# A four-layer graph network on one core: the third layer's weights' pass with its SyncE and ScalarE queues written out, and other points at which gathered rows are spilled

## The reference

```python
e = ei_all[idx_i] + ej_all[idx_j]
e = jnp.where(e > 0, e, LEAKY_SLOPE * e)
alpha = _segment_softmax(e.astype(jnp.float32), idx_j, n)
msgs = alpha[:, None] * x[idx_j]
out = jax.ops.segment_sum(msgs, idx_i, num_segments=n)
return jax.nn.relu(out)
```

## Time and profile before

| what | value |
|---|---|
| median of 3 runs | 4589.87 us (4589.16 to 4594.28) |
| span of the profiled execution | 5974.2 us |
| time of the profiled execution itself | not recorded apart from its span |
| GpSimd busy over the span | 3220.8 us, 54% |
| TensorE busy over the span | 2467.8 us, 41% |
| VectorE busy over the span | 2086.7 us, 35% |
| the third layer's stage, first gather to the next layer's first | 2800.66 to 4639.86 us of the span |

### The profile page before, as it was taken

The page is one execution under the profiler, slowest core; times in us unless marked ns, Lnnn a source line. Parts: engine busy times, 40 slices in busy tenths (PEclk is TensorE's granted clock), DMA queues, the critical chain, the costliest instruction groups (busy, mean ns, idle before and its releaser), DMA issues. The chain is left out here.

```text
span 5974.2 us, 63099 instructions
## 1 busy us (share of the span) xinstructions
PE 2467.8 (41%) x16441; PEld 2221.3 (37%) x16441; DVE 2086.7 (35%) x5443; ACT 830.0 (14%) x2496; POOL 3220.8 (54%) x3391
## 2 busy tenths in 40 slices
PE   2344444444333333332766666454566222222221
PEld 1333333333233333331666666344455222222220
DVE  4344434444122222222444344355544122222223
ACT  0111212122000000000322222000001011001112
POOL 3555555554566666664344444545443666666664
PEclk7555555555555555555555555566666556555555
DMA  4222222222122222223333333455555344434443
GB/s 102 57 60 60 61 58 60 59 61 57 41 47 47 47 49 47 48 47 63 115 110 108 107 108 115 130 162 162 162 164 160 93 117 116 108 108 112 112 116 82
DMA packets 427122, 543.15 MB, mean 91 GB/s; under 512 B 116266, under 2 KB 291966, under 8 KB 426862
## 3 DMA queue, kind: packets, MB, share of 16 engines
q1 hardware_dynamic: 311618, 311.80, 17.7%
q0 software_dynamic: 108064, 223.63, 16.6%
q10 hardware_dynamic: 7344, 6.61, 0.4%
HBM read 403.82 MB, written 142.41 MB: 91 GB/s over the span
## 5 line engine op out<-in xcount | busy, mean ns | idle before, releaser
L523 POOL DMA_INDIRECT G<-table,IC x2496 | 2362.6, 947 | 1571.7 <-issue 832.5
L2412 POOL DMA_INDIRECT G<-table,IC x448 | 433.1, 967 | 580.9 <-ACT IC L2271 425.1
L2818 DVE TENSOR_TENSOR_SCAN GW<-BIG,GW,PS 128x512 f32<-128x512 bf16 x208 | 266.2, 1280 | 962.9 <-DMA BIG<-run_mask 620.8
L2412 POOL DMA_INDIRECT G<-table2c,IC x384 | 367.3, 956 | 407.0 <-DMA rows_ahead<-G 148.8
L2780 PE MATMUL PS<-IDENT,GW 128*128 128x128 f32 x840 | 192.5, 405 | 862.3 <-issue 481.4
L1360 PE MATMUL PS<-SEL,G 128*128 128x96 f32 x1664 | 372.1, 417 | 358.1 <-DVE SEL L556 217.1
L1032 PE MATMUL PS<-SEL,GW 128*128 128x96 f32 x1664 | 382.4, 419 | 291.6 <-DVEq L1095 158.9
L1360 PEld LDWEIGHTS PS<-SEL,G 128*128 128x128 f32 x1664 | 359.7, 327 | 365.5 <-DVE SEL L556 220.1
L2780 PEld LDWEIGHTS PS<-IDENT,GW 128*128 128x128 f32 x840 | 158.9, 215 | 887.3 <-issue 495.6
L1032 PEld LDWEIGHTS PS<-SEL,GW 128*128 128x128 f32 x1664 | 356.4, 322 | 304.3 <-DVEq L1095 165.3
L2426 PE MATMUL PS<-BIG 128*128 128x49 f32 x1680 | 387.4, 408 | 60.7 <-issue 31.8
(11 more groups left out here) (314 smaller groups left out, 3749.1 us busy)
## 6 DMA issues: line engine op xcount, KB each, us to landing
rows_ahead<-G SPq DMA_DIRECT2D x104, 520.0 KB
running_max<-BIG SPq DMA_DIRECT2D x105, 512.0 KB
G<-table,IC POOLq DMA_INDIRECT x2944
GW<-source_in_block SPq DMA_DIRECT2D x160, 256.0 KB
ROWSF<-edge_places SPq DMA_DIRECT2D x209, 192.0 KB
BIG<-run_mask SPq DMA_DIRECT2D x104, 256.0 KB
ROWSF<-rows_ahead SPq DMA_DIRECT2D x26, 520.0 KB
SELTF<-rows_ahead SPq DMA_DIRECT2D x26, 520.0 KB
```

The source lines that it names most:

```text
L523: pool.indirect_dma_start(out=G[:, b, u, 0:width], out_offset=None, in_=table, in_offset=bass.IndirectOffsetOnAxis(ap=IC[:, b * U + u:b * ...
L2412: pool.indirect_dma_start(out=GS[:, b, u, 0:width], out_offset=None, in_=table, in_offset=bass.IndirectOffsetOnAxis(ap=IC[:, b * U + u:b * ...
L2818: v.tensor_tensor_scan(RM[:, q, h * 512:(h + 1) * 512], MB[:, q, h * 512:(h + 1) * 512], PS[2 * q + h][:], before, ALU.min, ALU.max).then_ ...
```

## The change

It replaces the loops of `sp_sums` and `act_sums` by straight Python loops over all 104 groups, and with them the fixed places of the spills and index copies by a table `sums_plan`. Pair p now stands after group ceil((20.3 (p + 1) - 10) / 21.2 x 4) - 1, for as many pairs as fall inside the pass: pairs 0, 1, 2, 3 after groups 1, 5, 9, 13, pair 6 after group 24, and so on to pairs 25 and 26 after groups 97 and 101. That is 27 pairs in the pass, where it was 26. The plan of the message pass begins with pair 27 and counts from 20.3 x (p - 27), so each pair stands where the pair two before it stood. The wait for the column moves from ScalarE's queue to GpSimd's, between the last gather from `T2` and the first from `T2C`.

```diff
+            FIRST_TURN, LEAD, EARLY = 21.2, 10.0, 28
+            sums_plan, plan, place = {}, {}, 0
+            for pair in range(EARLY):
+                at = max(0, math.ceil((PAIR * (pair + 1) - LEAD) / FIRST_TURN * RING) - 1)
+                if at < GROUPS:
+                    sums_plan.setdefault((at // RING, at % RING), []).append(pair)
+            kept_early = sum(map(len, sums_plan.values()))
+            for pair in range(kept_early, GROUPS // 2):
                 latest = (pair // 2, 1) if pair % 2 else (pair // 2 - 1, 3)
-                while points[place][0] < PAIR * (pair - 25) and points[place][1:] < latest:
+                while points[place][0] < PAIR * (pair - EARLY + 1) and points[place][1:] < latest:
...
+            def sp_sums(sp, reg):
+                for turn in range(LAPS):
+                    for b in range(RING):
+                        i = edge(turn, b)
+                        sp.wait_ge(lo_hot, i + 2)
+                        sp.dma_start(LOB[:, 1 - b % 2, :], LOD[(i + 1) * L:(i + 2) * L].unsqueeze(0)
+                                     .to_broadcast([P, L])).then_inc(lo_in[1 - b % 2], 16)
+                        sp.wait_ge(row_hot, i + 1)
+                        sp.wait_ge(terms, i + 1)
+                        load_windows(sp, reg, i, b % 2, T2W, 3, row_in, win_in)
+                        for pair in sums_plan.get((turn, b), ()):
+                            for group in (2 * pair, 2 * pair + 1):
+                                spill(sp, group, group % RING, group // RING)
...
-                        sp_sums(sp, reg, 0, 1, False)
-                        sp_sums(sp, reg, 1, LAPS // 2, True)
-                        spill(sp, 50, 2, 12)
-                        spill(sp, 51, 3, 12)
+                        sp_sums(sp, reg)
...
-                def refill(act, turn, b):
-                    for pair in plan.get((turn, b), ()):
-                        if pair == 26:
-                            act.wait_ge(column_in, 32)
+                            refill(act, sums_plan.get((turn, b), ()))
+
+                def refill(act, some):
+                    for pair in some:
...
                         gather_turns(pool, 0, PICKED // RING, T2, D)
+                        pool.wait_ge(column_in, 32)
                         gather_turns(pool, PICKED // RING, LAPS, T2C, C)
```

More of the change, by code:

```diff
@@ L1 @@
+import math
 import numpy as np
@@ L2250, in layer2 @@
                       for tau in range(LAPS) for b in (1, 3)]
-            plan, place = {}, 0
-            for pair in range(26, GROUPS // 2):
+            FIRST_TURN, LEAD, EARLY = 21.2, 10.0, 28
[6 more added lines that the diff above has]
+            for pair in range(kept_early, GROUPS // 2):
                 latest = (pair // 2, 1) if pair % 2 else (pair // 2 - 1, 3)
-                while points[place][0] < PAIR * (pair - 25) and points[place][1:] < latest:
+                while points[place][0] < PAIR * (pair - EARLY + 1) and points[place][1:] < latest:
                     place += 1
@@ L2344, in _ @@
                     sp.nop()
[L2346 to L2370, removed]
@@ L2372, in refill, with act_sums @@
-                def refill(act, turn, b):
-                    for pair in plan.get((turn, b), ()):
-                        if pair == 26:
-                            act.wait_ge(column_in, 32)
+                def act_sums(act):
+                    for turn in range(LAPS):
+                        for b in range(RING):
+                            i, q = edge(turn, b), b % 2
+                            k8 = (i + 1) * U
+                            act.wait_ge(z_ready, i + 2)
+                            a.activation(WE[:, q, :, 0], ZL[:, q, :, 0], ACT.Exp).then_inc(w_ready, 1)
+                            act.wait_ge(w_ready, i + 1)
+                            a.copy(NUM[:, k8:k8 + U], WE[:, q, :, 0])
+                            act.wait_ge(place_ready, i + 2)
+                            act.wait_ge(summed, i + 1)
+                            for u in range(U):
+                                ins = a.activation(PLACE[:, q, u, :],
+                                                   PS[3 + 2 * q + u // 4][:, (u % 4) * P:(u % 4 + 1) * P],
+                                                   ACT.Copy, scale=WE[:, q, u, 0:1])
+                            ins.then_inc(place_copied, 1)
+                            refill(act, sums_plan.get((turn, b), ()))
@@ L2385, in act_turns @@
                             copy_sums(act, S, n, blk, 2, False)
-                        refill(act, turn, 1)
+                        refill(act, plan.get((turn, 1), ()))
                         if n >= 0:
@@ L2390, in act_turns @@
                             copy_turned(act, S, n, 2)
-                        refill(act, turn, 3)
+                        refill(act, plan.get((turn, 3), ()))
                 @block.scalar
@@ L2397, in _ @@
                         start_acts(act, S)
[L2398 to L2401, removed]
+                        act_sums(act)
                         act_turns(act)
```

## The result

The changed kernel takes 4629.85 us (4629.36 to 4635.8, 4 runs) against 4592.07 us (4589.16 to 4598.61, 4 runs) of the kernel before. The ratio is 1.0083, 95% interval 1.0069 to 1.0097: 38 us slower, where 12 us faster was forecast. 4629.85 us lies outside the forecast range of 4561 to 4600.

A forecast was written before the change was run, and what follows sets the result against it. GpSimd's gathers were taken to bound the third layer: 1119 + 44 = 1163 us before; after, 1143, so the groups' 617 + 506 + 28 = 1151 ends it. Gain 12 us, forecast 4578 us, range 4561 to 4600.

The forecast's parts named there:

- The model of the weights' pass: Third layer's weights' pass: 5.45 us a group, group i done at 54 + 5.45 (i - 1) us from the first gather.
- the loops' removal: SyncE and ScalarE queues: by the skill's rule some 11 laps x 1 us gained on each; nothing expected.
- the plan releases them in time: Message pass: the last 24 pairs are released without GpSimd waiting, so they take 480 us.
- the slow rival: Weights' pass waits for its own spills if a group takes under 4.9 us; up to 20 us slower, 4610 us; chance 0.14.
- a pair of 20.0 us in the weights' pass: GpSimd's gathers: one every 1.25 to 1.28 us, so a pair of groups costs 20.0 us or slightly more.
- the column's landing: End of the weights' pass: 3 us, an estimate, from the column's store until GpSimd's wait ends at 619 us.
- The sum: Third layer's end: GpSimd 1163 us before and 1143 after, against 1151 us for the groups; gain 12 us.
- GpSimd's chain: Third layer's gathers on GpSimd, ending at 1119 us before and 1099 after; 44 us more to the next layer.
- the groups' chain: Message pass from 617 us, 506 us of groups, 28 us to the next layer: 1151 us, from 1130 to 1177.
- the 1180 that the prediction took for a bound: Most the timed third layer can take: 4590 - 290 outside the gathers - 3120 for three other layers.
- late turns: Last 12 turns of the message pass: 15.1 us each, up to 19 in neighbouring turns.
- The rival *no change: Third layer: groups already over 1160 us before, or GpSimd faster unprofiled, so its 20 us are slack; 4581 to 4599; chance 0.36.

The follow-up runs named there:

- the second profile: The kernel before, unchanged, profiled again: 4592.13 us, span 4590.3 us.
- The later plan: Kernel with straight code and the pairs' old places, its message pass's plan counted from 24.3, each pair 14 us later: 4586.92 us, ratio 0.9993.
- the neighbouring kernel with a pair each turn: Changed kernel with pair p behind group 4p + 1 in the weights' pass, message pass's plan counted from pair 25: 4586.8 us, ratio 1.0000.

## Why the prediction was wrong

**The model of the weights' pass** held: 5.45 us a group, pair 2 at 54 us after the first gather, pair 28 before at 643 where 639 was worked out, the column's store before at 615 where 616 was. Taking the undisturbed rows of a disturbed profile was right for the groups of this pass. Straight code costs nothing and brings nothing, as said (ratio 1.0003). The Trainium skill, "Runtime: NRT & Kernel Launch", section "Instruction fetch mechanics", says that a taken branch out of the two resident blocks forces a fetch; by it the prediction priced the loops' removal at some 11 us, then expected nothing of it, and the runs show nothing.

**The step that failed: the message pass's plan.** The prediction let "the plan releases them in time" stand for both kernels and asked only when GpSimd would be free. It did not ask what a spill costs that stands *too early*. Each pair's spill moved up by two pairs, 40.6 us of plan, while GpSimd gained 20 by my own sum and 4 in the trace. So SyncE came to most spills before the gathers (24 waits, 136.8 us, against 17 and 87.2), and the loads of the next groups stood behind. This is the mechanism of the slow rival (the queues wait for their own spills), but I placed it in the weights' pass alone, and gave it the condition of a group under 4.9 us. The two runs with only the plan changed out or in give 31 and 39 us for it. The sign that I had named for that rival, SyncE waiting at spills in a longer weights' pass, came as well. My condition for it was too strict: pair 26 was put in at 27 x 20.0 + 3 = 543, which leaves out the 14 us idle ahead of pair 2 and has the pair too short. In the trace its last gather ends at 596, and SyncE stands at its spill from 594 to 599.

**A mis-sized term: a pair of 20.0 us in the weights' pass.** It takes 21.5, and 21.8 from start to start. I read it where the profile had slowed VectorE: it has three of its 1024-element comparisons beside that pair, and eight beside a pair of the second profile. Even so those rows give 20.4 us (15 intervals in 19.16 us, times 16), of which I took 20.0. At points 20.9 us apart and pairs of 21.8, SyncE has to wait at each spill from pair 6 on. Cost: 12 us at the column's store (627 for 615), shown by the run that removes it with faster gathers.

**A second mis-sized term: the column's landing.** 3 us were taken; from the store to pair 28's first gather are 11.6 us in the changed kernel (SyncE's row, then GpSimd's):

```profile
2891.62 0.40 SPq L2336 DMA_DIRECT2D table2c<-VC  x1
```

```profile
2903.26 0.95 POOL L2395 DMA_INDIRECT G<-table2c,IC  x1 [20.61 <-issue]
```

The four other runs with 27 pairs in the weights' pass have 11.1 to 13.1 us. The store itself is 11 us later than forecast (627 for 616) and the landing 9 us longer, so that pair 28 begins at 638 and not at 619. Before it began at 643, and GpSimd keeps 4 us of its 20. In the run with straight code alone the wait's move to GpSimd did no harm.

**Which chain ends the layer.** The sum took GpSimd's chain as the bound before (1163 against 1151). The later plan lets GpSimd end 9 us later and the layer is no slower, and the runs in which GpSimd ends 10 to 26 us earlier gain at most 5: the groups' chain, with SyncE's waits in it, was the bound. It measured 1194 before, 43 us over the 1151 of the sum, and above the 1180 that the prediction took for a bound. That bound used idle times from the slowed profile, and they were shorter at real speed: 31 us between the first two layers' gathers in place of 49. Two terms of the groups' chain were too small. The message pass was let begin at 617, but its first selection is at 635, 20 us after the column's store; the prediction's own rows had 19.4 us for this. With 635 its sum would have been 635 + 506 + 28 = 1169, over the 1163 of GpSimd's chain, and the forecast gain would have been nothing. The other term is the message pass itself: from the first selection to the last group's sum it takes 531 us, with SyncE's waits in it, where 506 was taken. Its late turns take 17.1 us on average in both kernels; the row of their fourth group comes 15.1 and 19.3 us apart by turns in before's second profile, and the prediction had read the short one. The rival *no change* had this part right; had the plan of the message pass stayed, the result would have been 7 us slower, within the 9 us that it called no change.

The range, 4561 to 4600, rested on the cases that I had named. It missed because the slow case was looked for in the weights' pass only and not in the message pass.

The 38 us do not divide cleanly between the two parts: 12 and 25 at the landmarks, 7 and 31 by the runs. The parts need not add up, since the waits of the message pass depend on how late the weights' pass ends. With the old plan a store 13 us later costs only 7 us of the whole, as the message pass then takes 521 us instead of 526. Not settled is how much of the message pass's loss goes through SyncE's queue and how much through ScalarE's, which waits for gathers in the same places.

## What to carry to other kernels

In an in-order queue a wait has two wrong sides. Placed too late it starves the engine that it frees; placed too early it holds everything behind it, and the second may be the steeper side. Here 14 us later cost nothing, and 14 us earlier, on the neighbouring kernel with a pair each turn, cost 8 us. When a table of due times is shifted, compare the shift with what the producer really gains, and count every queue that stands at the table's points. When two chains are compared, take the start of each from a row too, and not only its pace. And where the span and the timed runs disagree, profile the kernel again before its rows are used for durations: a producer's duration can come out too short in a stretch in which its neighbours were slowed.

## What the runs showed of the hardware

A profiled execution can be off by 1384 us (5974 for 4590), and the next one of the same kernel, with the same number of instructions, by under 2 us. Indirect gathers issued by GpSimd take 0.94 us, but 1.15 to 1.5 while VectorE runs 1024-element bf16 comparisons from SBUF to SBUF; writing such a comparison as 1023 elements with unlike shapes of source and destination brought the gathers' mean in that pass from 1052 to 968 ns, at 0.48 us for the comparison as before and 0.20 us for the last element. A store of 128 x 49 pieces of 8 bytes into a table in DRAM took 11.1 to 13.1 us from its issue to the next gather of the engine that waited for it, in the five runs in which that wait came last, among this pass's other traffic.
